# Scores of the first block made inside the projection section; normalisation on ScalarE; first queries taken from their bank

## The reference

```
x_bar = mean(x, axis=0);  lQ = masked_x @ Wlq;  lK = x @ Wlk;  lV = x @ Wlv + blv      # x is layer-normed
local_scores = where(adj, lQ @ lK.T * scale, -1e9)
global_scores = (masked_x @ Wgq) @ (x_bar @ Wgk).T * scale;  es = masked_x @ Wes
max_score = maximum(max(local_scores, axis=1), global_scores, es)
le, ge, ee = exp(each - max_score);  denom = sum(le) + ge + ee
res = le / denom @ lV + ge / denom * gV + ee / denom * eV
x1 = x + maximum(res, masked_x)
out = x1 + FFN(layernorm(x1))      # attention matrix, 8 experts 256-1024-256 with gelu, last layer with gelu
```

## Time and profile before

| | us |
|---|---|
| median of 3 runs | 1153.24 (1149.43 to 1153.48) |
| profiled execution | 1154.27, span 1152.5 |
| busy: PE, DVE, POOL, ACT | 1063.9, 887.6, 723.8, 549.8 |
| values' store, 1 MB, issue to landing (median) | 5.1 |
| the adjacency's load, 256 KB | 3.6 |

### The profile page before, as it was taken

How to read it: one execution, slowest core, us unless ns; L and a number is a source line. 1 busy time by engine, 2 the same in 40 slices (tenths; PEclk the granted TensorE clock), 3 DMA queues, 4 the chain that set the end, 5 groups by cost and what they waited for, 6 DMA issues and landing times.

```text
span 1152.5 us, 16106 instructions
## 1 busy us (share of the span) xinstructions
PE 1063.9 (92%) x5060; PEld 886.5 (77%) x5060; DVE 887.6 (77%) x1545; ACT 549.8 (48%) x963; POOL 723.8 (63%) x715
## 2 busy tenths in 40 slices
PE   5567899999999999999999999998768899999997
PEld 3456688888888888888888888876666788898886
DVE  6976998888878878878978978978536766787662
ACT  3541044444445444444544444465636466665673
POOL 4646477678778777768768768676444355645551
PEclk8888999999999999999999999999989999999999
DMA  7985223443444434445434435467715546554521
GB/s 242 301 295 212 76 89 131 141 165 121 142 169 142 147 140 158 134 141 162 155 130 163 147 110 174 141 220 264 272 56 180 207 141 237 193 183 145 195 74 55
DMA packets 103557, 188.74 MB, mean 164 GB/s; under 512 B 10418, under 2 KB 42035, under 8 KB 103219
## 3 DMA queue, kind: packets, MB, share of 16 engines
q1 hardware_dynamic: 103474, 187.74, 48.2%
HBM read 147.81 MB, written 31.51 MB: 156 GB/s over the span
## 4 chain that ended last, share of the span: by engine, by line
PE 76%; DVE 8%; issue 3%; ACT 2%; POOL 2%; DMA 1%; DVEq 0%; POOLq 0%; ACTq 0%; SPq 0%
PE u_ps L1407 19%; PE s_ps L50 11%; PE s_ps L51 11%; PE s_ps L52 11%; PE u_ps L1414 9%; PE u_ps L50 2%; DVE scores L955 2%; PE u_ps L51 2%; PE u_ps L52 2%; DVE h_lo L1030 1%; PE mb_ps L50 1%; PE mb_ps L51 1%; PE mb_ps L52 1%; PE s_ps L1469 1%; PE mt_ps L51 1%
## 5 line engine op out<-in xcount | busy, mean ns | idle before, releaser
L840 POOL TENSOR_TENSOR p_lo<-p_all,p_hi 128x512 fp32r<-128x512 f32 x247 | 325.5, 1318 | 191.7 <-PE u_ps L1414 127.0
L1215 ACT ACTIVATE p_hi<-scores 128x512 fp32r<-128x512 f32 x256 | 161.7, 632 | 402.7 <-DVE scores L946 383.1
L1407 PE MATMUL u_ps<-p_hi,v_in 128*128 128x512 f32 x1024 | 278.8, 394 | 6.3 <-DMA v_in<-v_scratch 5.4
L955 DVE TENSOR_TENSOR scores<-s_ps,bias 128x512 f32<-128x512 f32 x256 | 175.7, 686 | 95.4 <-PE s_ps L52 94.1
L1407 PEld LDWEIGHTS u_ps<-p_hi,v_in 128*128 128x128 f32 x1024 | 192.2, 190 | 46.6 <-DMA v_in<-v_scratch 6.3
L50 PE MATMUL s_ps<-q_hi,lnT_hi 128*128 128x512 f32 x512 | 201.5, 394 | 8.4 <-POOL q_lo L845 6.9
L51 PE MATMUL s_ps<-q_lo,lnT_hi 128*128 128x512 f32 x512 | 199.9, 391 | 0.0
L52 PE MATMUL s_ps<-q_hi,lnT_lo 128*128 128x512 f32 x512 | 199.8, 390 | 0.0
L833 POOL TENSOR_SCALAR bias<-adj 128x512 f32<-128x512 uint8 x256 | 165.2, 645 | 24.7 <-DVE scores L955 22.7
L946 DVE TENSOR_TENSOR scores<-scores,mb_ps 128x512 f32<-128x512 f32 x256 | 171.6, 676 | 0.8 <-PE mb_ps L1431 0.8
L969 DVE TENSOR_TENSOR kept_ps<-kept_ps,scores 128x512 f32<-128x512 f32 x232 | 162.2, 699 | 8.0
(11 more groups left out here) (178 smaller groups left out, 1660.9 us busy)
## 6 DMA issues: line engine op xcount, KB each, us to landing
v_in<-v_scratch SPq DMA_DIRECT2D x128, 512.0 KB, 3.7
adj<-in_adj SPq DMA_DIRECT2D x64, 256.0 KB, 3.6
raw<-in_wffn SPq DMA_DIRECT2D x32, 512.0 KB, 4.8
v_scratch<-vst SPq DMA_DIRECT2D x8, 1024.0 KB, 5.1
xg<-in_x SPq DMA_DIRECT2D x8, 512.0 KB, 5.9
mg_raw<-in_mxT SPq DMA_DIRECT2D x16, 256.0 KB, 3.6
q_scratch<-q_out SPq DMA_DIRECT2D x16, 256.0 KB, 5.1
q_raw<-q_scratch SPq DMA_DIRECT2D x8, 512.0 KB, 4.6
```

The costliest lines, as they stand in the source:

```text
L840: nc.gpsimd.tensor_tensor(out=p_lo[:, y % 2], in0=p_all[:, y % 2], in1=p_hi[:, y % 3].bitcast(fp32), op=ALU.subtract).then_inc(plo_ready, 1)
L955: nc.vector.tensor_tensor(scores[:, t % SLOTS], s_ps[t % 3][:, :], bias[:, t % 2], ALU.add).then_inc(masked, 1)
L1215: nc.scalar.activation(p_hi[:, y % 3], scores[:, y % SLOTS], ACT.Exp, scale=SCALE).then_inc(phi_ready, 1)
L1407: nc.tensor.matmul(u_ps[d][:, :], v_in[:, i % VRING, x % 2, at:at + P], p_hi[:, x % 3], start=k == 0 and part == 0, stop=False)
```

## The change

The two blocks become one; the order of all engines is written out for g = 0 to 8, without the hardware loop. In turn g the keys of group g are made, the queries of group g, and the scores of the four tiles of group g-1 against the queries of block 0 (tiles t to t+3 with t = 4g-4). The later loops begin at step 32.

- The queries of block 0 aren't stored and loaded: ACT takes `q_hi` and DVE `q_lo` from the bank. The load of block 1's queries stands behind all seven stores.
- ACT normalises (`normalise`: scale = 1/deviation, bias = `nmr` = -mean/deviation; `nmr` is one small DVE operation, `shift`). `lnf` and `vst` have one buffer instead of two.
- All buffers of the section lie under ring slots 15 to 36, the ring's lower slots take scores at once; the banks are shared with the later ones.
- The weights are split in between (ACT and POOL, turns 0 to 2) and stored in turn 3 ahead of that turn's values. The row products of block 0 are made in turns 5 and 6 (own term) and after the section (global term).

```diff
+        qw = under_slot(15, 15)("qw", [P, KD, D])
+        w_all = under_slot(16, 19)("w_all", [P, 4, KD, D])
+        w_low = under_slot(20, 23)("w_low", [P, 4, KD, D], fp32r)
+        w_high = under_slot(24, 27)("w_high", [P, 4, KD, D], fp32r)
+        xg = under_slot(28, 31)("xg", [P, 2, TG, D])
+        lnf = under_slot(32, 33)("lnf", [P, TG, D])
...
+        tr_ps, q_ps = u_ps, [mb_ps, mt_ps]
+        qw_ps, gw_ps, attc_ps = s_ps
...
-                    dve.wait_ge(rstd_ready, g + 1)
-                    for j in range(TG):
-                        last = nc.vector.tensor_scalar(lnf[:, pp, j, 1:D], xg[:, pp, j, 1:D], mv[:, pp, j, 0:1], rstd[:, pp, j:j + 1],
-                                                       ALU.subtract, ALU.mult)
-                    last.then_inc(ln_ready, 1)
...
+                def group(g):
+                    if g == 0:
+                        sp.wait_ge(qw_done, 1)
+                        for n, w in enumerate((wgkT, wgqT)):
+                            sp.dma_start(wq_in[:, n], kblocks(w)).then_inc(wg_loaded, 16)
...
+                    if g + 2 < NG:
+                        sp.wait_ge(ln_ready, g + 1)
+                        load_x(g + 2)
+                    if g + 2 < NG:
+                        sp.wait_ge(q_done, 2 * g + 2)
+                        load_masked(g + 2)
+                    if g == 3:
+                        sp.wait_ge(wlo_ready, 4)
+                        sp.dma_start(whi_dram, w_high[:, :, :, :].bitcast(fp32)).then_inc(w_stored, 16)
+                        sp.dma_start(wlo_dram, w_low[:, :, :, :].bitcast(fp32)).then_inc(w_stored, 16)
+                    if g == 4:
...
+                    sp.wait_ge(vlo_ready, g + 1)
+                    sp.dma_start(v_dram[g * TG:(g + 1) * TG].rearrange("t p c -> p t c"), vst[:, :, :].bitcast(fp32)).then_inc(v_stored, 16)
+                    if g > 0:
+                        sp.wait_ge(q_copied, 2 * g)
+                        sp.dma_start(q_dram[g], q_out[:, :, :]).then_inc(q_stored, 16)
+                    if g + 1 > 1:
+                        wait(sp, bias_ready, 4 * g)
+                        load_adjacency(sp, g + 1)
...
+                sp.wait_ge(q_stored, 16 * (NG - 1))
+                load_queries(sp, 1)
+                load_masked_rows(sp, 1, 0)
                 sp.wait_ge(v_stored, 16 * NG)
+                sp.wait_ge(q_done, 2 * NG)
...
+                for g in range(NG + 1):
+                    t = 4 * g - 4
+                    if g < NG:
+                        low_values(g)
+                    if g + 1 < NG:
+                        reciprocal_deviation(g + 1)
+                    if g == 0:
+                        low_weight_matrix(0)
+                        low_weight_matrix(1)
+                    if g > 0:
+                        bias_of(t + 2)
+                    if g + 1 < NG:
+                        low_masked_half(g + 1)
+                    if g == 2:
+                        low_weight_matrix(2)
+                        low_weight_matrix(3)
+                    if g > 0:
+                        bias_of(t + 3)
+                    if g == NG:
+                        low_queries(1, 0)
+                        low_queries(1, 1)
+                        bias_of(t + 4)
+                    else:
+                        bias_of(t + 4)
+                        bias_of(t + 5)
+                for t in range(KT, STEPS):
...
+                for g in range(NG + 1):
+                    t = 4 * g - 4
+                    if 0 < g and g + 1 < NG:
+                        first_moments(g + 1)
+                    if g < NG:
+                        for k in range(KD):
+                            low_turned(g, k)
...
+                    for i in range(4):
+                        if g > 0:
+                            mask(t + i)
+                            keep(t + i)
+                        if i == 0 and g + 1 < NG:
+                            shift(g + 1)
+                        if i == 1 and g == NG:
+                            dve.wait_ge(xbar_added, 1)
+                            nc.vector.tensor_scalar(xbar_c[0:1, 0], mb_ps[0:1, 0:P], -1.0, 1.0, ALU.mult, ALU.add).then_inc(xbar_fixed, 1)
+                        if i == 2 and g + 1 < NG:
+                            low_masked_half(g + 1)
...
+                    if g == 0:
+                        for k in range(KD):
+                            dve.wait_ge(q0hi_ready, k + 1)
+                            nc.vector.tensor_tensor(q_lo[:, 0, k], q_ps[k][:, :], q_hi[:, 0, k].bitcast(fp32), ALU.subtract).then_inc(qlo_ready, 1)
+                        dve.wait_ge(attc_done, 1)
+                        dve.wait_ge(rows_loaded, 16 * 3)
...
+                dve.wait_ge(rows_loaded, 16 * 5)
+                dve.wait_ge(rows_done, 1)
+                nc.vector.tensor_copy(wg_b[:, :], mt_ps[:, D:2 * D]).then_inc(row_ready, 1)
+                nc.vector.tensor_tensor(gv_b[:, :], mt_ps[:, 0:D], gv_b[:, :], ALU.add).then_inc(row_ready, 1)
+                dve.wait_ge(row_ready, 1)
+                for j in range(TG):
+                    first_extra(j, wg_b, mb_ps[:, j % 2 * D:(j % 2 + 1) * D], 1.0, 0, TG + j + 1)
+                top_extra(0)
+                for t in range(KT, STEPS):
...
+                def normalise(g):
+                    act.wait_ge(nmr_ready, g + 1)
+                    act.wait_ge(ones_ready, 1)
+                    wait(act, tr_done, 2 * g)
+                    wait(act, vlo_ready, g)
+                    for j in range(TG):
+                        last = nc.scalar.activation(lnf[:, j, 1:D], xg[:, g % 2, j, 1:D], ACT.Identity, scale=rstd[:, g % 2, j:j + 1],
+                                                    bias=nmr[:, g % 2, j:j + 1])
+                    last.then_inc(ln_ready, 1)
...
+                for g in range(NG):
+                    act.wait_ge(ln_ready, g + 1)
+                    wait(act, v_stored, 16 * g)
+                    nc.scalar.activation(vst[:, :, 0:D], lnf[:, :, :], ACT.Copy).then_inc(vhi_ready, 1)
+                    for k in range(KD):
+                        act.wait_ge(tr_done, 2 * g + k + 1)
+                        nc.scalar.activation(lnT_hi[:, k, g * CH:(g + 1) * CH], tr_ps[k][:, :], ACT.Copy,
+                                             accum_out=xsum[:, k, g:g + 1]).then_inc(thi_ready, 1)
+                    if g == 0:
+                        for k in range(KD):
+                            act.wait_ge(q_done, k + 1)
+                            nc.scalar.activation(q_hi[:, 0, k], q_ps[k][:, :], ACT.Copy).then_inc(q0hi_ready, 1)
+                    if g + 1 < NG:
+                        normalise(g + 1)
+                        high_masked_group(g + 1)
+                    if g == 0:
+                        act.wait_ge(w_loaded, 64)
+                        high_weight_matrix(WEV)
+                        high_weight_matrix(WNEXT)
+                        act.wait_ge(gw_done, 1)
+                        nc.scalar.activation(wq_in[:, 0], gw_ps[:, :].rearrange("p (k n) -> p k n", k=KD), ACT.Copy).then_inc(gw_ready, 1)
...
+                    if g > 0:
+                        wait(act, q_stored, 16 * (g - 1))
+                        for k in range(KD):
+                            act.wait_ge(q_done, 2 * g + k + 1)
+                            nc.scalar.activation(q_out[:, k, :], q_ps[k][:, :], ACT.Copy).then_inc(q_copied, 1)
+                high_queries(1)
...
+                def turn_keys(g):
+                    pe.wait_ge(ln_ready, g + 1)
+                    wait(pe, tlo_ready, 2 * g)
+                    for k in range(KD):
...
+                for g in range(NG + 1):
+                    t = 4 * g - 4
+                    if g < NG:
+                        turn_keys(g)
+                    if g == 0:
+                        pe.wait_ge(qwlo_ready, 1)
+                        queries(0, 0)
+                        queries(0, 1)
+                        pe.wait_ge(wg_loaded, 32)
+                        fold(gw_ps, gw_done)
...
+                    if g == 1:
+                        pe.wait_ge(gw_ready, 1)
+                        pe.wait_ge(attcol_ready, 1)
+                    if g > 0:
+                        score(t)
+                        if g < NG:
+                            queries(g, 0)
+                        score(t + 1)
+                        if g < NG:
+                            queries(g, 1)
+                        if g == NG:
+                            pe.wait_ge(xbar_ready, 2)
+                            pe.wait_ge(q_copied, 2 * NG - 2)
+                            for k in range(KD):
+                                last = nc.tensor.matmul(mb_ps[:, 0:P], ones[:, :], xbar_c[:, k], start=k == 0, stop=k == KD - 1)
+                            last.then_inc(xbar_added, 1)
+                        score(t + 2)
+                        score(t + 3)
+                pe.wait_ge(wg_loaded, 48)
+                pe.wait_ge(xbar_fixed, 1)
```

(3 more changed lines are left out.)

531 lines of the change are left out of this document (216 added, 315 removed).

## The result

The changed kernel takes 1138.14 us (median of 4 runs, 1137.27 to 1141.2) against 1153.05 us for the kernel before on the same chip: a ratio of 0.9877, 95% interval 0.9859 to 0.9895. The profiled execution took 1137.43 us (span 1135.6), 16.8 us less than the profiled execution before; 18.2 had been forecast. The first weighing of values starts at 134.25 instead of 151.41, 17.16 us sooner, and from there to the end of the span both need the same time: 1001.1 us before, 1001.35 after. So everything that follows is about the first 134 us.

The account below looks back on a forecast made before the run. Time could be won only ahead of 146 us, in DVE-paced opening turns and a score stage bound by DVE and PE. Tile 32's mask moves from 143.44 to 125.2: 1154.27 - 18.2 = 1136.1 us; range 1118 to 1151.

Parts of the forecast that it names:

- Start: Opening section before the turns: first queries at 14.2 us, then weights, masked rows and biases until 28.9.
- first D: D is the moment DVE begins a turn; the first was put at 28.9 us, with no mask sooner.
- The ring: Opening-section turns: DVE, ACT and POOL wait on one another in a circle, 11.3 us a turn; main forecast, chance 0.50.
- Rival B: Opening-section turns: DVE's own work sets them, 9.4 us each, half the single costs hide; 1119 us, chance 0.18.
- The single costs: Extras in the turns: low weights 2.5, weight stores 3.0, small loads 1.5, row products 2.2; together 9.2 us.
- Rival D: Single vst buffer: store landings from 8.6 us set the turn; with 12 us, slower than before, 1163 us; chance 0.08.
- Rival C: Opening-section turns of 12.3 to 13 us from store landings of 7 to 10.7 or slower normalisation; 1144 us, chance 0.17.
- The end of the section: Last D to mask of tile 32: 20.5 us through block 1's query store and load; DVE alone 16.4.
- From mask 32 to the first weighing: Behind the opening section: same order in both kernels, so 7.97 us as before.
- The sum: D of group 7 at 104.7 plus 20.5 gives tile 32's mask at 125.2; gain 18.2 us.
- The clock: PE's clock in the turns: high level (2.4 GHz) from turn 2 on; end of the section starts low.

Follow-up runs that it names:

- edit 1: Changed kernel with ACT making mg_hi ahead of the normalisation; ratio 0.9803 to the kernel before.
- edit 8: edit 6 plus row products behind the turn's low keys and the subtraction from the value weights in turn 1; 1122.39 us, ratio 0.9729 to the kernel before.
- edit 6: Changed kernel with mg_hi ahead of the normalisation and the values' store ahead of all loads but x; ratio 0.9757 to the kernel before.
- edit 2: Changed kernel with the values' store issued ahead of the weight stores and small loads; ratio 0.9815 to the kernel before.
- edit 7: Changed kernel with the four row products of turns 5 and 6 moved behind the turn's second mask; ratio 0.9866 to the kernel before.
- edits 2 and 10: edit 2 has its own line; 10 is the changed kernel with edit 7's moved products and the early load of block 1's queries, ratio 0.9842.
- edits 3, 7 and 9: edit 3 and edit 7 have their own lines; 9 is the changed kernel with block 1's queries loaded early, in turn 5, ratio 0.9883.
- edit 3: Changed kernel with the four wes row products moved from turns 5 and 6 to behind the section; ratio 0.9881 to the kernel before.
- edit 4: Changed kernel with DVE normalising again instead of ACT, in the new order of work; ratio 0.9878 to the kernel before.

## Why the prediction was right, and where its steps were not

- **Start.** First queries 14.30 (forecast 14.2), first D 27.66 (28.9). Right within 1.2. POOL was ready before D; what set D was DVE's wait of 3.91 for mg_hi and its subtraction from the value weights, 2.90 for two beside POOL's low weights and 0.75 ahead of them (edit 1), which the forecast had not priced. Moving it into turn 1 (edit 8) gave nothing that shows: turn 2 begins at 37.7 there and at 37.0 in edit 6.
- **The ring.** Right in its order and its size: 11.3 in turn 3, and edit 1 breaks it where the forecast put it. The normalisation was 2.07, not 1.7.
- **Rival B (DVE-bound, 9.4)** was wrong for this kernel and is what edit 1 makes of its turn 3: 8.86.
- **The single costs** are a step that failed: 9.2 forecast. The six turns took 84.1 us; six of 11.3 less 1.2 are 66.6; so 17.5. The low weights in turn 2 are right (14.0 long for 13.8). The four products were put at 2.2 and took 6.0 with their readouts: two of them took 2.5 instead of 0.42, 4.2 more, since the forecast laid them beside nothing while POOL's vst operation starts with them. The value stores were put at 4.5 and cost 7.1, what turns 4 and 5 are above 11.3 without the products (2.9 and 4.2); edit 2 takes 7.0 out of the turns. What the late stores cost shows a turn after the issue. The last 1.7 are turn 1: it was to be 1.2 shorter than the ring for want of a maximum of tile 0 and was 0.5 longer, as DVE stood 0.71 us for POOL's deviation there.
- **Rival D's mechanism**, the one vst buffer that decides from a landing of 8.6, is there in two of eight stores (10.6 and 9.0) and not in the median (6.0). That is why it cost some 7 us and not 28. **Rival C** named the same landings, but as a ring of 12.3 to 13 us in every turn; the undisturbed turn kept 11.3, and its time (1144) did not come.
- **The end of the section** erred the other way: D+15.8, not D+20.5. DVE alone had been put at D+16.4, near what came; the step that failed is that the query path ends later. The stretched product had put off D of the last turn itself, and the last queries were copied before it (store issued at 111.91, D+0.1 instead of D+3.5); the load landed in 3.6 instead of 5.0, and PE had work until the score and did not start low. With the products out of the way (edit 7, D at 106.13) the path does end the section, at D+18.1: store at D+3.2, landed 5.3 later, load 3.4, low queries 2.67, score at the low level, with DVE's products, stretched by these low queries, only 0.3 us ahead.
- **From mask 32 to the first weighing** 6.6 us instead of 7.97. In the kernel before, PE stood 1.55 us for the block's maximum (143.57) and had scores left to make when the first exponentials were ready (149.71): it weighed 1.7 us later. Here it had made more scores ahead, and weighed 0.75 us after them (133.50).
- **The sum:** 1.2 sooner, 8.3 more in the turns, 4.7 less at the end, 1.4 less behind it: +1.0 on the forecast first weighing of 133.2 (125.2 and 7.97). The time is right because errors of opposite sign nearly cancel, not because each step was: that the sum came out within 1 us is luck. The ring itself, 11.3 us of each turn, was forecast rightly.
- **The clock.** Full level was forecast from turn 2 on, because the low one had been seen after 4.41 us without work and not after 3.40. It came back in turn 3, behind waits of 2.36 and 1.06 us. The length of the pauses alone does not tell it: with 2.34 and 1.11 to 1.20 us the same transposes are low in edits 2 and 10 too (1.97), with 2.33 to 2.38 and 1.23 to 1.25 they are high in edits 3, 7 and 9 (1.09), and behind 2.35 us the next turn's are high in edit 3 (74.80) and low in edit 7 (75.16). What else it needs, no run here tells. And it cost nothing there: turn 3 is 11.31 to 11.33 us long in all six. The Trainium skill, "TensorE: Matmul & The Clock Gate", section "What's actually happening", has the low clock as the default that activity lifts; these rows agree as far as they show both levels.

## What to carry to other kernels

Look in each engine's order for a step that needs nothing from the instruction it stands behind: here one swap of two lines on ScalarE took 2.4 us from an undisturbed turn, because a third engine waited for the second of them. Count per turn what such an edit brings: of its 6.7 us, 5.2 came in front of the turns. A staging buffer with one copy makes the landing of its store part of the loop, so its store belongs ahead of every transfer that nobody is waiting for. And where two chains end together, remove both before judging either: the early load brought nothing alone, and 4.0 us between the last D and the first weighing once the products were out of the way. Equal times need not mean that an engine is indifferent: edit 4 replaced a ring of 11.3 us by 11.2 us of DVE's own work.
